# Attention values turned on VectorE instead of TensorE, and expert tables written in three steps

## What is computed

```python
def _token_diffusion(x, Wqk, Wv, Wo, tau):            # H = 16 heads of 16
    qk = (x @ Wqk).reshape(b, n, H, dh).transpose(0, 2, 1, 3)
    v = (x @ Wv).reshape(b, n, H, dh).transpose(0, 2, 1, 3)
    dot = jnp.einsum('bhnd,bhmd->bhnm', qk, qk)
    logits = (2.0 * dot - q2[..., :, None] - q2[..., None, :]) / math.sqrt(dh)
    attn = jax.nn.softmax(logits * tau, axis=-1)
    out = jnp.einsum('bhnm,bhmd->bhnd', attn, v)
    return out.transpose(0, 2, 1, 3).reshape(b, n, d) @ Wo
...
x = x + _token_diffusion(_layernorm(x, ln1_w, ln1_b), ...) * gamma1
x = x + _channel_diffusion(_layernorm(x, ln2_w, ln2_b), ...) * gamma2   # 8 heads of 32 channels
...
logits = xf @ w_router
topk_w, topk_idx = jax.lax.top_k(jax.nn.softmax(logits), 2)
h = gelu(jnp.einsum('te,ieh->tih', xf, w1) + b1)      # hidden width 1024
out = jnp.einsum('tih,ihe->tie', h, w2) + b2          # weighted by topk_w, summed
```

## Time and profile before

| what | value |
|---|---|
| median of 3 executions | 1119.0 us (1118.0 to 1121.36) |
| the profiled execution | 1118.23 us, of which the span is 1116.4 us |
| PE busy | 1032.4 us, 92% of the span |
| DVE busy | 671.4 us, 60% |
| ACT busy | 721.1 us, 65% |
| POOL busy | 384.5 us, 34% |
| the eight batches start at | 32.0, 76.4, 136.2, 202.5, 268.8, 335.1, 401.5, 468.0 us |
| attention ends, unit 0 starts | about 533, 538.3 us |

### The profile page before, as it was taken

How to read it: one execution, slowest core, us unless ns; L and a number is a source line. 1 busy time by engine, 2 the same in 40 slices (tenths; PEclk the granted TensorE clock), 3 DMA queues, 4 the chain that set the end, 5 groups by cost and what they waited for, 6 DMA issues and landing times. The chain is left out here.

```text
span 1116.4 us, 17406 instructions
## 1 busy us (share of the span) xinstructions
PE 1032.4 (92%) x5756; PEld 702.8 (63%) x5756; DVE 671.4 (60%) x1902; ACT 721.1 (65%) x1106; POOL 384.5 (34%) x353
## 2 busy tenths in 40 slices
PE   5899999999999999998899996999999999989966
PEld 3234545555455455544588875888888888878842
DVE  5225265454735645354785777677677776679927
...
GB/s 267 133 246 61 264 31 204 122 84 256 18 261 73 174 150 69 275 148 91 147 100 115 62 135 123 124 133 148 147 161 119 138 143 142 151 143 224 149 215 256
DMA packets 48960, 167.47 MB, mean 150 GB/s; under 512 B 10160, under 2 KB 16688, under 8 KB 42864
## 3 DMA queue, kind: packets, MB, share of 16 engines
...
q10 hardware_dynamic: 150, 0.41, 0.2%
...
## 5 line engine op out<-in xcount | busy, mean ns | idle before, releaser
L589 ACT ACTIVATE E<-PS,VV 128x1024 f32<-128x1024 f32 x256 | 271.6, 1119 | 73.7 <-PE PS L974 72.6
L1737 PE MATMUL PH<-XP,W1P 128*128 128x512 f32 (+1 forms) x1104 | 233.1, 369 | 4.9 <-DVE HP L1678 4.5
L1737 PEld LDWEIGHTS PH<-XP,W1P 128*128 128x128 f32 x1104 | 185.8, 192 | 44.5 <-DVE HP L1678 8.1
L974 PE MATMUL PS<-OPB,OPA 102*128 102x512 bf16 x512 | 137.9, 386 | 11.4 <-DMA OPB<-norm_parts 5.7
L1678 DVE TENSOR_TENSOR HP<-PH,HP 128x512 fp32r<-128x512 f32 x156 | 106.7, 686 | 64.8 <-ACT HP L1584 64.3
L957 PE MATMUL PO<-E,VA 128*32 128x512 f32 x1024 | 143.5, 610 | 0.0
L1579 ACT ACTIVATE PH<-PH,B 128x512 f32<-128x512 f32 (+1 forms) x184 | 107.5, 596 | 53.9 <-PE PH L1737 44.9
L1502 POOL DMA_INDIRECT choice_rows<-Y,DI x78 | 79.3, 1016 | 182.3 <-DVE Y L1635 160.8
L974 PEld LDWEIGHTS PS<-OPB,OPA 102*128 102x128 bf16 x512 | 37.7, 98 | 155.4 <-ACT E L589 68.7
L1570 ACT CAST W2P<-WG 128x512 fp32r<-128x512 f32 x92 | 56.9, 621 | 103.6 <-PE PB L1768 63.6
...
L1767 PE MATMUL PY<-W2P,HP 128*128 128x512 f32 x288 | 110.6, 412 | 5.0 <-DVE Y L1635 5.0
...
## 6 DMA issues: line engine op xcount, KB each, us to landing
...
```

Source lines behind the costliest of these rows:

```text
L589: a.activation(E[:, s % 2, h, :, :], PS[:, u % 2, :, :], ACT.Exp, scale=vec("tau_t")[:, 4 * (s // 2) + h:4 * (s // 2) + h + 1]).then_inc(e ...
L974: ins = t.matmul(PS[:, u % 2, jc, :], OPA[0:KA, m, key:key + P], OPB[0:KA, m, hh * N:hh * N + N], start=True, stop=True)
L1737: last = m.matmul(PH[:, u % BANKS, at:at + w], W1P[:, a, k * HID + c * P:k * HID + c * P + P], XP[:, o, k, 0:w], start=(k == 0 and (a, o) ...
```

## The change

The output weights are loaded with their rows in another order, 16 rows at a time, so that the heads' values may stay where a transpose of 32x32 blocks puts them. DVE then does the whole of `untok`: two transposes of 128x512 of `OT` into `Z3T`, one reciprocal, two products of 256 columns into `ON`, one transpose into `OTN`, for each half m. The PE steps `untok0`, `untok1`, `ontok` and ACT's `ontok` are gone, and `proj` waits for `otn_ready`. `untok0` is at position 1, `untok1` at 2, and every step from `proj` on is one position earlier.

`fill_begun` has two stages: stage 0 as before, with 20 dependent instructions, and stage 1 of 26 at slot 17, for units 5 and 6, when seven batches are counted. `BEGUN` is 7, so units 5 and 6 take the three separate matmuls, and `fill_tables` serves units 7 on. The last batch's steps stand from slot 19 to slot 75, where they stood from 18 to 52.

```diff
-BEGUN = -(-(2 * N * (B - 2) - NE * (2 * SUB - 1)) // (2 * SUB))
+KNOWN = [-(-(2 * N * b - NE * (2 * SUB - 1)) // (2 * SUB)) for b in (B - 2, B - 1)]
+BEGUN = KNOWN[-1]
...
-PRE_USES, POST_USES, LATE_USES = 7, 18, 4
+PRE_USES, POST_USES, LATE_USES = 7, 12, 4
...
-POST_AT = {2: ['residual', 'untok0'], 3: ['untok1'], 4: ['ontok'], 5: ['proj'], 6: ['z2'], 8: ['x2t'], 9: ['qkc'], 10: ['gram'],
-           11: ['dist'], 12: ['soft_c'], 13: ['weights_c'], 14: ['mix'], 15: ['weff']}
+POST_AT = {1: ['untok0'], 2: ['residual', 'untok1'], 4: ['proj'], 5: ['z2'], 7: ['x2t'], 8: ['qkc'], 9: ['gram'],
+           10: ['dist'], 11: ['soft_c'], 12: ['weights_c'], 13: ['mix'], 14: ['weff']}
...
-           5: [('chan_stats', B - 2), ('ontok', B - 1)], 7: [('proj', B - 1)], 8: [('chan_norm', B - 2)], 9: [('z2', B - 1)],
+           5: [('chan_stats', B - 2)], 7: [('proj', B - 1)], 8: [('chan_norm', B - 2)], 9: [('z2', B - 1)],
...
-           17: [('prefix', B - 2)], 18: [('x2t', B - 1)], 20: [('qkc', B - 1)], 22: [('gram', B - 1)], 24: [('dist', B - 1)],
...
-           43: [('z3t1', B - 1)], 44: [('logits', B - 1)], 45: [('soft', B - 1)], 46: [('top', B - 1)], 50: [('prefix', B - 1)],
-           52: [('tables', B - 1)]}
+           17: [('prefix', B - 2), ('begin', B - 2)], 19: [('x2t', B - 1)], 22: [('qkc', B - 1)], 25: [('gram', B - 1)],
...
+           57: [('z3t0', B - 1)], 59: [('z3t1', B - 1)], 61: [('logits', B - 1)], 63: [('soft', B - 1)], 65: [('top', B - 1)],
+           71: [('prefix', B - 1)], 75: [('tables', B - 1)]}
...
-            sp.dma_start(WB[:, :, :, :], wview[:, 2:6]).then_inc(w_rest, 16)
+            sp.dma_start(WB[:, 1:4, :, :], wview[:, 3:6]).then_inc(w_rest, 16)
+            for h in range(H // KC):
+                q, g = h % 4, h // 4
+                at = 32 * q + DH * g
+                sp.dma_start(WB[at:at + DH, 0, :, :], wview[DH * h:DH * h + DH, 2]).then_inc(w_rest, 16)
...
-                    at_least(act, post_full, POST_USES * (b - 1) + C)
+                    at_least(act, otn_ready, KC * b)
...
-            def untok(half):
+            def untok(m):
                 def step(b, par):
...
-                    if half == 0:
+                    if m == 0:
                         post.at(b)
-                    for c in (2 * half, 2 * half + 1):
-                        ps = takep(b, c).rearrange("p (h e) -> p h e", e=32)
-                        post.did(v.reciprocal(REC[:, c, :], ps[:, :, DH]))
-                        post.wait()
-                        v.tensor_tensor(ON[:, c, :].rearrange("p (h e) -> p h e", e=DH), ps[:, :, 0:DH],
-                                        REC[:, c, :].unsqueeze(2).to_broadcast([P, H, DH]), ALU.mult).then_inc(post_free[c % 2], 1)
+                    dve.wait_ge(po_read, GROUPS * b + 2 * m + 2)
+                    for r in range(2):
+                        post.did(v.transpose(TK[:, r, :], OT[:, 2 * m + r, :]))
+                    post.wait()
+                    blocks = TK[:, :, :].rearrange("p r (j e) -> p r j e", e=32)
+                    post.did(v.reciprocal(REC[:, :, :], blocks[:, :, :, DH]))
+                    post.wait()
+                    for r in range(2):
+                        post.did(v.tensor_tensor(TN[:, m, :].rearrange("p (j r d) -> p r j d", r=2, d=DH)[:, r], blocks[:, r, :, 0:DH],
+                                                 REC[:, r, :].unsqueeze(2).to_broadcast([P, N // 32, DH]), ALU.mult))
+                    post.wait()
+                    v.transpose(OTN[:, m, :], TN[:, m, :]).then_inc(otn_ready, 1)
...
                 if isinstance(b, int) and b == B - 3:
-                    fill_begun(nc, dve, table_links, begun_ready, COUNT, const, QR[:, :, :].rearrange("p k n -> p (k n)"), TAKEN, tables)
+                    fill_begun(nc, dve, table_links, begun_ready, COUNT, const, QR[:, :, :].rearrange("p k n -> p (k n)"), TAKEN, tables, 0)
+                if isinstance(b, int) and b == B - 2:
+                    fill_begun(nc, dve, table_links, begun_ready, COUNT, const, OT[:, :, :].rearrange("p g n -> p (g n)"), TAKEN, tables, 1)
...
-                emptied(pe, b, 4)
-                emptied(pe, b, 5)
-                rows_times(b, 6, OTN, lambda k: mat(wo, k))
+                pe.wait_ge(otn_ready, KC * (b + 1))
+                rows_times(b, 0, OTN, lambda k: mat(wo, k))
...
+            if t == KNOWN[0]:
+                sp.wait_ge(begun["begun_ready"], 2)
             if t == BEGUN:
                 sp.wait_ge(tables_ready, 1)
```

More of the change, by code:

```diff
@@ L1223, in subtile_of, with fill_begun @@
     return first_block(t) // HALVES
-LINKS_BEGUN = 20
-def fill_begun(nc, dve, table_links, begun_ready, COUNT, const, free, TAKEN, tables):
+def fill_begun(nc, dve, table_links, begun_ready, COUNT, const, free, TAKEN, tables, stage):
     v, ALU, AX = nc.vector, mybir.AluOpType, mybir.AxisListType
     RI, WI, OK, DUMP, FE = tables
-    U, at = BEGUN, [0]
+    lo, hi = KNOWN[stage - 1] if stage else 0, KNOWN[stage]
+    U, at = hi - lo, [0]
     def take(*shape):
@@ L1239, in take @@
         return flat if len(shape) == 1 else flat.rearrange("p (a b) -> p a b", a=shape[0])
-    linked = [0]
+    linked = [LINKS_BEGUN[stage - 1] if stage else 0]
     def link(i):
@@ L1248, in fill_begun @@
     rows_of, most = COUNT[:, 0, :], STEPS_E // 2 - 1
-    over, full, start, ends = take(NE, most), take(NE), take(NE), take(NE)
+    over, full, start, ends, ahead = take(NE, most), take(NE), take(NE), take(NE), take(NE)
     cube, held = take(NE, NE), take(U, NE)
@@ L1254, in fill_begun @@
     link(v.reduce_sum(full, over, AX.X))
+    if stage:
+        link(v.tensor_tensor(full, full, TAKEN[:, :], ALU.subtract))
+        link(v.tensor_tensor(ahead[:, 0:NE - 1], TAKEN[:, 1:NE], TAKEN[:, 0:NE - 1], ALU.subtract))
+        link(v.memset(ahead[:, NE - 1:NE], 0.0))
+        link(v.tensor_tensor(ahead, full, ahead, ALU.subtract))
     link(v.tensor_tensor(cube, full.unsqueeze(1).to_broadcast([P, NE, NE]),
@@ L1264, in fill_begun @@
     link(v.reduce_sum(expert, held, AX.X))
-    link(v.tensor_tensor(held, held, full.unsqueeze(1).to_broadcast([P, U, NE]), ALU.mult))
+    link(v.tensor_tensor(held, held, (ahead if stage else full).unsqueeze(1).to_broadcast([P, U, NE]), ALU.mult))
     link(v.reduce_sum(passed, held, AX.X))
     link(v.tensor_tensor(passed, unit, passed, ALU.subtract))
+    if stage:
+        link(v.tensor_scalar(passed, passed, TAKEN[:, 0:1], None, ALU.add))
+    link(v.tensor_scalar(start, start, -1.0, float(U), ALU.mult, ALU.add))
+    link(v.tensor_tensor(start, start, full, ALU.min))
+    if stage:
+        link(v.tensor_scalar(start, start, 0.0, None, ALU.max))
+        link(v.tensor_tensor(TAKEN[:, :], TAKEN[:, :], start, ALU.add))
+    else:
+        link(v.tensor_scalar(TAKEN[:, :], start, 0.0, None, ALU.max))
     link(v.scalar_tensor_tensor(place, expert, float(TOK // (2 * SUB)), passed, ALU.mult, ALU.add))
```

123 lines of the change are left out of this document (48 added, 75 removed).

## The result

The changed kernel takes 1136.9 us (median of four, 1134.2 to 1137.9) where the kernel before takes 1118.5: a ratio of 1.015, 95% interval 1.012 to 1.018. Every ratio here is estimated, with its interval, from the executions in the fast state alone, and can differ by up to 0.002 from the ratio of the two medians beside it. The forecast was 1110. The profiled execution took 1136.83, its span 1134.9, which is 18.5 more than before.

A forecast was written before the change was run, and what follows sets the result against it. PE, busy 92% of the span, was taken as the bound, with DVE becoming it in middle batches. Middle batches -8.0, batch 1 -4.0, batch 7 +1.5 and tables +2.3 gave -8.2 from 1118.23: 1110 us, range 1100 to 1124.

The forecast's parts named there:

- A transpose of 128x512 on VectorE: In untok: each new DVE transpose takes 0.69 us, priced as a sum of the same size.
- Rival D: Batches 0 to 6: DVE transposes cost more than a sum; at 1.08 each, 1126 us; chance 0.15.
- The tables' chain: Expert units: the chain's cost moves from unit 3 (-13.3 us) to unit 4 (+12.3, bounds +8 and +15).
- a granted clock below 1.00 in batches 2 to 6: Middle batches: a sign that would show the forecast wrong; no size given.
- `z3t0` waited 0.80 for VectorE: Middle batches: PE waiting about 1.5 to 2 us for DVE at z3t0 was a sign of being right.
- the collision: Middle batches: untok1's products beside POOL's residual take up to 1.3 us more each; 0.9 taken, bounds 0 and 2.6.
- A middle batch, step by step: Batches 2 to 6: DVE becomes the bound, so each gains 1.6 us, not 4.8; five batches -8.0.
- rival C: Middle batches: PE's clock halves behind its waits, costing 1.7 us each, five times 8.5; 1118.5, no change; chance 0.15.
- `chan_stats` and `split0` now queue behind `proj`'s sum: Middle batches, DVE: from proj's second sum to the end of np's copy takes 10.3 us with gaps.
- The last batch: Batch 7: half of some 3 us more DVE work on untok shows, +1.5 us (bounds -2 and +4).
- Unit 0: First expert unit: small changes of both signs taken as nothing; units 0 and 2 between -1.5 and +1.5 us.
- Unit 5: Expert unit 5 loses the joined matmul, +0.3 us; the clock's dip of 2.5 was counted in unit 4.

The follow-up runs named there:

- e9_tail: e8_lastpost with the last batch's untok0, untok1, proj and z2 at unit slots 4, 6, 8, 11 instead of 3, 4, 7, 9: 1108.8 us, ratio 0.990.
- e5b_order: Only the change's values part, with untok1 at position 1 and chan_stats and split0 at 3 instead of 4: 1114.1 us against 1118.3 for the kernel before, ratio 0.9945.
- e8_lastpost: e5b_order's kernel with later places for the last batch's post steps, and the other batches' transposed values in QR: 1105.9 us against 1118.3 for the kernel before, ratio 0.987.

## Why the prediction was wrong

**Right.** A transpose of 128x512 on VectorE: 0.69 forecast, 0.69 measured. No row showed one; the price was that of a sum of the same size on the same engine, with 0.47 and 1.08 as rows on both sides, so that it came out this close is in part luck. The estimate of 1.24 us by the Trainium skill's page "VectorE: DVE Perf Modes" (The three transpose paths), four tiles of 311 ns, does not fit this instruction; the measurement decides. Rival D, which priced them at 0.89 or more, was not what made the kernel slower. Batch 4 ran as the working has it up to `untok1`: `untok0` ended at T + 10.8 (10.6), `chan_add` at 13.5 (13.3). From the second sum of `proj` to the copy's end 10.05 (10.3). The tables' chain lost in unit 4 what it gained in unit 3, -12.6 and +11.2 for -13.3 and +12.3. Of the signs that the prediction named for being wrong, one came: a granted clock below 1.00 in batches 2 to 6. `z3t0` waited 0.80 for VectorE, where 1.5 to 2 was to show the forecast right.

**The step that failed first** is the collision in "A middle batch, step by step". The products were given 0.9 us more, with 0 and 2.6 as bounds, and the sum took the middle. It was 2.56. The trace of before had the reason in it. POOL in batch 4 of the kernel before:

```profile
280.52 0.19 POOL L447 COPY SM<-MU 128x4 f32 x1 [3.05 <-DVE X L825]
...
281.02 1.89 POOL L450 TENSOR_TENSOR X<-X,SM 128x1024 f32<-128x1024 f32 x1 [0.19 <-POOL SM L448]
283.00 1.89 POOL L453 TENSOR_TENSOR X<-X,SM 128x1024 f32<-128x1024 f32 x1
```

`residual` is released by the last sum of `chan_add` (`L825`), and the changed order put `untok1` exactly behind `chan_add`. Both start together, and POOL's two sums of 1.89 back to back cover both products, so the upper bound was the value.

**The second** is rival C, held for a rival where it belonged to the sum. Its reason against, that the clock stayed at 1.00 behind a wait of 0.79, did not carry to longer waits. Behind waits of 2.10 to 2.38 the clock fell in three of four batches, 1.7 us each; e9_tail shows falls of 1.6 us behind waits of 1.02. Late half (+2) and, where the clock fell, slower `proj` (+1.8) brought `z3t0` of batch 4 to T + 35.0 instead of 31.4. Five batches came out 11.5 us above the forecast; 5 of these are the three falls.

**The third** is that the sum took the order of the steps as given and asked only what VectorE costs in it. The prediction said that `chan_stats` and `split0` now queue behind `proj`'s sum, and drew no wait from it but a lost gain. e5b_order shows that these two positions and untok1's were all that stood between +0.7 and -2.2 us a middle batch.

**Mis-sized terms.** The last batch, +4.2 for +1.5: the products collide there too, PE waited 5.28 for `OTN`, and the chain to `prefix` has all of untok ahead of it; e8_lastpost, with half of untok behind `chan_norm`, has the 70.4 of before. Unit 0, +3.5 for 0 ("small changes of both signs"): VectorE was busy 34.0 of 39.9 us there (its window above), fuller than any window of the earlier trace rows, and has 38.5 now, 1.7 of them collision (the products of untok0 took 2.46 there). Unit 5, +2.8 for +0.3: the clock stood at half for 13.7 us around the end of the tables' wait of 10.45, the last 5 of them in unit 5, where 2.5 us of dip were counted in unit 4 alone.

**Not in the prediction at all**: the drain, 7.5 us. Without it the changed kernel would be at about 1129, above the range as well.
